# Moving the second layer norm's scaling from VectorE to ScalarE, and the down projection's low part from VectorE to GpSimd

## The reference

```python
x = layernorm(x + linear_attention(x, Wq, Wk, Wv, Wo, Wa, ba))      # 16 heads of 64, decaying state
x = layernorm(x + cross_attention(x, ctx_1024, mask, ...))           # 16 heads of 16, 77 keys
x = layernorm(x + mixture_of_experts(x, ...))                        # 8 experts, 2 per row, 256 -> 512 -> 256, silu(g) * u
def layernorm(x): return (x - mean(x)) / sqrt(var(x) + 1e-5)
```

## Time and the profile before

| | |
|---|---|
| device time, median of 3 runs | 1602.39 us (1598.70 to 1604.08) |
| the profiled execution: its time, its span | 1602.39 us, 1600.6 us |
| PE / PEld busy | 1336.9 / 1126.1 us (84% / 70%) |
| DVE / ACT / POOL busy | 893.8 / 867.3 / 745.6 us (56% / 54% / 47%) |
| granted TensorE clock, mean | 0.915 |

### The profile page before, as it was taken

One profiled execution on the slowest core, in us unless ns is written; L12 is line 12 of the kernel. 1 busy time (PEld: TensorE's weight loads), 2 busy tenths in 40 slices (PEclk: granted clock), 3 DMA queues, 4 the chain that ended last, 5 costly groups with the idle time before them and its releaser, 6 DMA issues. The chain is left out here.

```text
span 1600.6 us, 30942 instructions
## 1 busy us (share of the span) xinstructions
PE 1336.9 (84%) x10439; PEld 1126.1 (70%) x10439; DVE 893.8 (56%) x1838; ACT 867.3 (54%) x1922; POOL 745.6 (47%) x824
## 2 busy tenths in 40 slices
PE   5999999999999999997788888723799999998200
PEld 4788888888888888885566666523688988887200
DVE  3344445444444444452678888769355555566446
ACT  4677777777777777775155545400455455455101
POOL 2244444444444444454377777601554444444464
PEclk9999999999999999998899999855799999999655
DMA  3200000000000000000223233202354554455234
GB/s 125 75 15 21 21 15 21 21 21 15 21 21 21 15 21 21 8 21 28 67 69 98 74 86 84 63 26 83 117 168 144 164 171 147 147 169 176 83 114 131
DMA packets 123554, 116.40 MB, mean 73 GB/s; under 512 B 42242, under 2 KB 104298, under 8 KB 123434
## 3 DMA queue, kind: packets, MB, share of 16 engines
q1 hardware_dynamic: 116618, 96.23, 19.6%
q0 software_dynamic: 6816, 18.62, 4.3%
HBM read 83.93 MB, written 24.07 MB: 67 GB/s over the span
## 5 line engine op out<-in xcount | busy, mean ns | idle before, releaser
L290 POOL TENSOR_SCALAR_AFFINE_SELECT a_decay<-a_decay 128x256 f32<-128x256 f32 x256 | 113.7, 448 | 259.9 <-ACT a_decay L370 259.9
L493 DVE TENSOR_TENSOR a_probs<-a_ps_s,a_decay 128x384 f32<-128x384 f32 x256 | 131.6, 552 | 164.4 <-PE a_ps_o L668 152.8
L299 POOL TENSOR_TENSOR a_key_sum<-a_probs 128x256 f32<-128x256 f32 x128 | 94.5, 738 | 170.3 <-DVE a_probs L493 159.2
L333 ACT ACTIVATE a_qk_exp<-a_ps_qk 128x512 f32<-128x512 f32 x128 | 76.6, 599 | 136.7 <-PE a_ps_qk L574 129.4
L486 DVE SCALAR_TENSOR_TENSOR a_qk<-a_qk_exp,a_qk_relu 128x512 f32<-128x512 f32 x128 | 89.3, 698 | 105.8 <-ACT a_qk_relu L334 105.7
L574 PE MATMUL a_ps_qk<-a_xT_hi,a_w_hi 128*128 128x256 f32 x512 | 145.0, 283 | 3.6 <-ACT a_qk_relu L334 3.6
L1753 POOL TENSOR_TENSOR e_gu_lo<-e_gu_raw,e_gu_hi 128x2048 fp32r<-128x2048 f32 x23 | 106.5, 4629 | 83.6 <-ACT e_gu_hi L1773 83.6
L574 PE MATMUL a_ps_qk<-a_xT_hi,a_w_lo 128*128 128x256 f32 x512 | 143.8, 281 | 0.0
L574 PE MATMUL a_ps_qk<-a_xT_lo,a_w_hi 128*128 128x256 f32 x512 | 143.8, 281 | 0.0
L649 PE MATMUL a_ps_s<-a_qk 64*128 64x256 f32 (+1 forms) x1024 | 131.7, 338 | 0.5 <-DVE a_probs L493 0.2
L1746 POOL DMA_INDIRECT e_x_in<-x_rows,e_index x78 | 75.0, 962 | 121.0 <-DVE e_index L1849 104.0
(11 more groups left out here) (281 smaller groups left out, 4064.1 us busy)
## 6 DMA issues: line engine op xcount, KB each, us to landing
e_gu_raw<-in_L_ffn_gate_w SPq DMA_DIRECT2D x23, 512.0 KB
e_gu_raw<-in_L_ffn_up_w SPq DMA_DIRECT2D x23, 512.0 KB
e_dn_raw<-in_L_ffn_down_w SPq DMA_DIRECT2D x23, 512.0 KB
y_sorted<-e_y_out SPq DMA_DIRECT2D x16, 512.0 KB
a_x_in<-in_x SPq DMA_DIRECT2D x16, 256.0 KB, 2.7
a_x_res<-in_x SPq DMA_DIRECT2D x16, 256.0 KB, 2.7
x_rows<-a_x SPq DMA_DIRECT2D x16, 256.0 KB, 2.1
b_x_in<-x_rows SPq DMA_DIRECT2D x16, 256.0 KB
```

The lines of the kernel that those rows point to most:

```text
L290: pool.affine_select(out=d, in_=d, compare_op=ALU.is_ge, fill=0.0, base=0, pattern=[[0, 2], [1, P]], channel_multiplier=-1)\
L299: pool.tensor_tensor(key_sum[:], probs[:, :, P:N], probs[:, :, N:TRI], ALU.add).then_inc(keys_summed, 1)
L333: act.activation(qk_exp[:], ps_qk[:], ACT.Exp)
L493: vec.tensor_tensor(probs[:, h, :], ps_s[h][:, 0:TRI], decay[h][:], ALU.mult)\
```

## The change

In cross attention `scale_x2` is taken out of VectorE. ACT's `root(b)` becomes `normalise(b)`: ln, exp, a third instruction for -1/sqrt, two one-column instructions for shift = mean * (-1/sqrt), and then x2 = Identity(resid * rstd + shift), twice 128x256. The two waits of `scale_x2` (for the stores of x2 and for its transposes, both of the sequence before) move with it to ACT, and the call moves in ACT's order from behind `keep_q` to ahead of `keep_pT(b-1, 1)`. In experts `dn_low` is taken out of VectorE; GpSimd makes `e_dn_lo` right behind `e_gu_lo`, ahead of the gathers, also for tile 0.

```diff
-            def root(b):
+            def normalise(b):
                 act.wait_ge(var_ready, b + 1)
                 act.activation(ln_var[:], mv[:, :, 1], ACT.Ln, bias=eps_col[:]).then_inc(rstd_step, 1)
-                act.wait_ge(rstd_step, 2 * b + 1)
+                act.wait_ge(rstd_step, 4 * b + 1)
+                act.activation(rstd[:], ln_var[:], ACT.Exp, scale=-0.5).then_inc(rstd_step, 1)
+                act.wait_ge(rstd_step, 4 * b + 2)
+                act.activation(minus_rstd[:], rstd[:], ACT.Copy, scale=-1.0).then_inc(rstd_step, 1)
+                act.wait_ge(rstd_step, 4 * b + 3)
+                for blk in range(NB):
+                    ins = act.activation(shift[:, blk:blk + 1], mv[:, blk, 0:1], ACT.Copy, scale=minus_rstd[:, blk:blk + 1])
+                ins.then_inc(rstd_step, 1)
+                act.wait_ge(rstd_step, 4 * b + 4)
                 if has(b, -1):
-                    act.wait_ge(x2_ready, b)
-                act.activation(rstd[:], ln_var[:], ACT.Exp, scale=-0.5).then_inc(rstd_step, 1)
+                    act.wait_ge(x2_stored, 32 * b)
+                    act.wait_ge(x2T_made, b)
+                for blk in range(NB):
+                    ins = act.activation(x2[:, blk, :], resid[:, blk, :], ACT.Identity, bias=shift[:, blk:blk + 1],
+                                         scale=rstd[:, blk:blk + 1])
+                ins.then_inc(x2_ready, 1)
...
                 if has(b, 1):
                     keep_xT(b + 1)
+                if has(b, -2):
+                    normalise(b - 2)
                 if has(b, -1):
                     keep_pT(b - 1, 1 - par, 1)
                 if has(b, 1):
                     keep_q(b + 1)
-                if has(b, -2):
-                    root(b - 2)
...
-            def scale_x2(b):
-                vec.wait_ge(rstd_step, 2 * b + 2)
-                if has(b, -1):
-                    vec.wait_ge(x2_stored, 32 * b)
-                    vec.wait_ge(x2T_made, b)
-                for blk in range(NB):
-                    ins = vec.tensor_scalar(x2[:, blk, :], resid[:, blk, :], mv[:, blk, 0:1], rstd[:, blk:blk + 1],
-                                            ALU.subtract, ALU.mult)
-                ins.then_inc(x2_ready, 1)
...
             def low_parts(par, turn):      # GpSimd, experts
                 pool.tensor_tensor(gu_lo[par][:], gu_raw[par][:], gu_hi[par][:].bitcast(F32), ALU.subtract)\
                     .then_inc(gu_lo_done[par], 1)
+                pool.wait_ge(dn_hi_done[par], turn + 1)
+                pool.sem_inc(pool_turns, 1)
+                pool.tensor_tensor(dn_lo[par][:], dn_raw[par][:], dn_hi[par][:].bitcast(F32), ALU.subtract)\
+                    .then_inc(dn_lo_done[par], 1)
...
-            def dn_low(par, turn):         # VectorE, experts
-                vec.wait_ge(dn_hi_done[par], turn + 1)
-                vec.sem_inc(vec_turns, 1)
-                vec.tensor_tensor(dn_lo[par][:], dn_raw[par][:], dn_hi[par][:].bitcast(F32), ALU.subtract)\
-                    .then_inc(dn_lo_done[par], 1)
...
                 for f in range(2, FC):
                     hidden(f)
                     hid_low(f)
-                if has(t, 1):
-                    dn_low(1 - par, turn + par)
```

More of the change, by code:

```diff
@@ L784, in cross_attention @@
         ln_var, rstd = sb("b_ln_var", [P, NB]), sb("b_rstd", [P, NB])
+        minus_rstd, shift = sb("b_minus_rstd", [P, NB]), sb("b_shift", [P, NB])
         x2, x2T = sb("b_x2", [P, NB, D]), sb("b_x2T", [P, KC, N])
@@ L1069, in _ @@
             keep_oT(B - 1)
-            root(B - 2)
+            normalise(B - 2)
             keep_x2T(B - 2)
-            root(B - 1)
+            normalise(B - 1)
             keep_x2T(B - 1)
@@ L1153, in sequence @@
                 sums(b, par, 0)
-                if has(b, -2):
-                    scale_x2(b - 2)
                 if has(b, 1):
@@ L1173, in _ @@
             all_sequences(vec, sequence)
-            scale_x2(B - 2)
             add_residual(B - 1)
             statistics(B - 1)
-            scale_x2(B - 1)
             keep_logits(B - 2)
@@ L1647, in run_experts @@
         where_loaded, sp_turns, pool_turns = sem("e_where_loaded"), sem("e_sp_turns"), sem("e_pool_turns")
-        vec_turns = sem("e_vec_turns")
         w_loaded, b_loaded = sems("e_w_loaded"), sems("e_b_loaded")
@@ L1903, in _ @@
             x_low(0, 0)
-            dn_low(0, 0)
             all_tiles(vec, tile)
```

## The result

The change makes the kernel slower: 1627.33 us median (1623.96 to 1629.72, 4 runs) against 1600.55 us (1598.70 to 1604.08), ratio 1.0152, 95% interval 1.0131 to 1.0175. By the ratio that is +24.4 us of 1602.39 where +18 was forecast (the two medians lie 26.8 apart); 1627 lies in the range of 1603 to 1636.

A forecast was written before the change was run, and what follows sets the result against it. The prediction took a loop through several engines to bound cross attention, with PE full in experts' 512-row tiles. From 1602.39 us, +13 (x2 on ACT), +2.4 and +2.5 (e_dn_lo on GpSimd) made +18: 1620 us, range 1603 to 1636.

The forecast's parts named there:

- The loop of a pass: Cross attention: one pass through PE, ACT and VectorE takes 16.66 us at full clock, 0.52 above the mean before.
- `normalise` 2.2 us: Cross attention, ACT: normalise, now ahead of keep_pT, takes 2.2 us between keep_xT and keep_pT; bounds 1.8 and 2.6.
- The clock, 0.55 us a pass: Cross attention: PE's idling ahead of project_q lowers the clock under 0.90, costing 0.55 us a pass; bounds 0 and 1.4.
- Part 1 in all, +13: Cross attention, x2 on ACT: 17.2 us a pass, 1.06 more, over twelve passes +13 us; bounds +1 and +28.
- Start of experts, +2.4: Start of experts: VectorE's one-hot table instructions stand still again while GpSimd makes e_dn_lo(0), +2.4 us without cover.
- Large tiles, nothing: Experts, 512-row tiles: gathers slide by two microseconds, but PE needs the rows only in the next tile; no cost.
- Small tiles, +2.5: Experts, 256-row tiles: e_dn_lo gets between the two hid_low, 12.25 us a tile (10.95 if behind both); +2.5 us taken.
- The stores of x2: Cross attention, rival: the wait for x2's stores, now at ACT, takes over if landing is late; 1633 us, chance 0.10.
- The rival that VectorE's release wins: Cross attention: VectorE was the bound, so freeing it makes the kernel faster if normalise is short; 1596 us, chance 0.08.
- The rival of an unharmed clock, 1611 us: Slower ACT without clock loss: 0.52 us a pass, +6 in cross attention and +3 in experts; 1611 us, chance 0.12.
- Part 2: Experts, e_dn_lo on GpSimd: +2.4 us at the start and +2.5 in the 256-row tiles, nothing in the 512-row tiles.

The follow-up runs named there:

- e3: e1 with normalise(b-2) moved behind keep_q(b+1) in ACT's order, same work; 1593.16 us, ratio 0.9936 to the kernel before.
- e4: e1 with normalise's pair of 128x256 instructions doubled into an unread spare buffer; 1662.24 us, ratio 1.0373 to the kernel before.
- e1: Changed kernel with dn_low back on VectorE, so only x2 on ACT remains; 1616.46 us, ratio 1.0092 to the kernel before.
- e5: e2 with the e_dn_lo of tile 0 alone given back to VectorE; 1592.79 us, ratio 1.0026 to the kernel before.
- e2: Kernel before with only dn_low moved to GpSimd, x2 work left as it was; 1610.10 us, ratio 1.0056.
- e6: e5 with e_dn_lo of the 256-row tiles also back on VectorE, GpSimd making it only during 512-row tiles; 1589.36 us, ratio 1.0007 to the kernel before.
- e12: Whole changed kernel, with normalise(b-2) moved behind keep_q(b+1) in ACT's order; 1586.47 us, ratio 0.9989 to the kernel before.
- e8: Kernel before with one added wait: GpSimd starts add_bias(b-1) only when VectorE has made x2 (b-2); 1581.28 us, ratio 0.9955.
- e9: e3 run again unchanged, on the same chip as e10 and e11; 1579.49 us, ratio 0.9937 to the kernel before.
- e10: e9 with ACT's keep_pT(b, 0) swapped ahead of exponentials(b, 1); 1588.91 us, ratio 0.9996 to the kernel before.
- e11: e10 with keep_logits(b-2) moved ahead of statistics(b-1) in VectorE's order; 1588.11 us, ratio 1.0000 to the kernel before.

## Why the prediction was right, and where its sizes were off

The direction and the loop of a pass came out as reasoned. Two steps failed, the clock and the large tiles.

- *The loop of a pass.* Forecast 16.66 us at full clock; the pass from 899.98 has 16.72. `turn_x1` to `project_q` 4.47 forecast, 4.49 measured; from there to the scores 4.56 and 4.56, to VectorE's reading 0.88 and 1.06, to the next `turn_x1` 6.75 and 6.61. e3 shows that this stretch is the cause, and e4 that what is added to it costs at least its own length.
- *`normalise` 2.2 us.* Mis-sized: 901.12 to 903.67 is 2.55. The pair takes 593 ns a piece in the mean, and not the 470 of the earlier trace rows; shift 0.48 and not 0.35. The formula of the Trainium skill (ScalarE: Activation LUTs, "What ACT_TABLE_LOAD costs") gives an estimate of 585 for such an instruction. The trace agrees. It came out even because the steps overlap: `normalise` starts 1.14 us behind `turn_x1` where 1.36 was counted, and `keep_pT` starts 0.10 ahead of its end.
- *The clock, 0.55 us a pass.* This step failed, by the prediction's own sign ("I am wrong if the clock does not fall"). From the first to the last of the twelve `turn_x1` the clock is 0.95, where the kernel before has 0.92; it did not fall under 0.90, it rose. Six of the eleven passes have 1.00 and one 0.99. The passes stand 17.10 us apart, 0.38 above the one of 16.72, and as the seven at full clock take 16.80 in the mean, only 0.30 of that goes with the clock. That two microseconds of idle time in each pass must cost clock was too simple. With 1.1 us more work at that place every pass did have a low clock (e4), but no run shows the rule.
- *Part 1 in all, +13.* Stage A grew by 12.9 us, and by 13.0 in e1. That the number fits is in part luck: the eleven intervals between the `turn_x1` grew by 10.6 us where 1.06 a pass would be 11.7, and what comes behind the last one by 2.3 (46.8 to 49.1), of which about one belongs to the twelfth pass and the rest to the tail of the stage, which was put at nothing.
- *Start of experts, +2.4.* The long e_col_hot group is 8.32 us (6.21 before), e_dn_lo 2.34; stage B +2.1, and e5 takes 2.4 back from e2.
- *Large tiles, nothing.* This step failed. The gathers slide behind e_dn_lo, as the prediction said, but PE does not have a whole tile of time for them: it waits at 1298.53, and the large tiles take 2.0 us more in the mean of the five kernels named at e6, 1.3 of them seen as such waits. Whether gathers ahead of e_dn_lo would save it wasn't tried.
- *Small tiles, +2.5.* About right, by terms that were a little off; the stretch behind them was not counted. `hidden(2)` stands 13.3 and 10.7 us apart in turn (1438.71, 1452.02, 1462.70, 1476.01): where e_dn_lo follows e_gu_lo at once it holds the pair up to 1451.37, and in the next tile it comes late and blocks `hid_low(2)`, 1.49 us in place of 0.43. Both cases occur in turn, at 13.3 and 10.7 where the forecast had 12.25 and 10.95. Five intervals take 61.1 us in the mean of the changed kernel, e2, e5 and e12 (59.8 to 62.3), and 58.2 in that of the nine without (57.1 to 60.6): +2.9. What comes behind them up to the memset is 1.4 longer.
- *Rivals.* The stores of x2 are no wait: b_x idles 0.17 us, for b_shift. The rival that VectorE's release wins failed at this place by the term named against it; at e3's place it is the truth, 9 to 10 us better. The rival of an unharmed clock, 1611 us, had the clock right and the time wrong: its 0.52 us a pass sets a full-clock pass against a mean of the kernel before that holds slow passes as well, where 0.96 was measured, and experts took over 8 us more where it had 3.

Part 2 was forecast at +4.9 and measured +9.0 (e2's ratio; 6 to 12 by its interval); its rows make 2.4 + 2.0 + 2.9 + 1.4 = 8.7. Part 1 was forecast at +13 and measured +14.7 (0.0092 of 1602; 12 to 17.5). These are the 6 us by which the forecast fell short: above all the large tiles and what comes behind the small ones, 3.4 together; the rest is no larger than the intervals.

## What to carry to other kernels

Where an engine's in-order queue feeds another one's, the place of the added work decides first and its amount second: look for the gap in which the engine waits anyway, and count what stands behind the new instructions up to the next engine. Before VectorE's work is moved because it looks long, ask how much of it is waiting for GpSimd: here one wait on GpSimd (e8) gave 7 of the 10 us that moving the work to the right place did (e3). A full engine that waits for nothing can still be reached through a DMA queued behind the moved work. The fastest kernel found is e3: x2 on ACT, but behind `keep_q`, and e_dn_lo left on VectorE, 9 to 10 us under the kernel before.

## What the runs showed of the hardware

- GpSimd and VectorE: several kinds of VectorE instruction with their operands in SBUF stand still until the GpSimd instruction at work is done, and one instruction of each gets in between two of the other. In the changed kernel the pair of `hid_low` takes 4.73 us (1446.64) and 0.76 alone (1436.53), and the cast of e_index, 0.15 us alone (1461.40), took 2.32 (1473.12) while e_dn_lo ran. Not every kind is held: the sum of the softmax weights, a reduction from SBUF to SBUF, takes 1.43 us beside GpSimd's instruction, as the maximum of the same shape takes 1.44 while GpSimd is idle (909.21 in e4). The kernel before, timelines of DVE and POOL:

```profile
913.26 1.43 DVE L1116 TENSOR_REDUCE b_den<-b_probs 128x16 f32<-128x1232 f32 x1
913.43 2.27 POOL L955 TENSOR_TENSOR b_probs<-b_probs,b_top 128x1232 f32<-128x1232 f32 x1 [0.98 <-DVE b_top L1111]
```

- The clock depends on more than the idle time in sum. Kernels with the same work have 0.96, 0.93 and 0.92 in this stage (e9, e10, e11), and e10, with 0.2 us less in a pass at full clock, is 9 us slower than e9.
- The final combination, 64 gathers by index on GpSimd, takes 91 us on three chips and 104 to 107 on another. In the kernel before, where it takes 104, the trace has this gap, while in the changed kernel, where it takes 91, GpSimd goes on without a stop:

```profile
1551.74 0.95 POOL L2007 DMA_INDIRECT f_y<-y_sorted,slots  x1 [0.30 <-issue]
1559.04 0.95 POOL L2007 DMA_INDIRECT f_y<-y_sorted,slots  x1 [6.36 <-DVE f_stats L2041]
```

(the kernel before, GpSimd's timeline). The gap is half of the 13 us; the other half lies behind the last gather, from whose end to the end of the span it is 16.3 us, and 9.4 in the changed kernel. The cause was not looked into.
